# Cross-attention and FP4 feed-forward: the gated rows' lowered block reciprocals computed by ScalarE instead of GpSimd

## What is computed

```python
def fp4_quant_dequant(x):                       # BLOCK = 16, along the last dim
    xb = x.reshape(shape[:-1] + (shape[-1] // BLOCK, BLOCK))
    scale = jnp.max(jnp.abs(xb), axis=-1, keepdims=True) / 6.0
    scale = jnp.maximum(scale, jnp.float32(1e-12))
    xn = xb / scale
    idx = jnp.searchsorted(_MID, jnp.abs(xn))
    q = _GRID[idx] * jnp.sign(xn) * scale
    return q.reshape(shape)

def fp4_linear(x, w):
    return jnp.einsum('bsk,nk->bsn', fp4_quant_dequant(x), fp4_quant_dequant(w))

x = x + xattn(layernorm(x), ctx_1024, ...)
n = layernorm(x)
h = silu(fp4_linear(n, w_gate)) * fp4_linear(n, w_up)      # 704 gated columns
x = x + fp4_linear(h, w_down)
```

## Time and profile before

| | before |
|---|---|
| median of 3 runs | 435.14 us |
| the profiled execution | 436.2 us |
| its span | 434.4 us |
| busy: TensorE matmul / weight load | 363.0 / 277.7 us |
| busy: VectorE | 352.0 us |
| busy: ScalarE | 276.5 us |
| busy: GpSimd | 213.7 us |
| mean granted TensorE clock | 0.96 of 2.4 GHz |

### The profile page before, as it was taken

How to read it: one execution, slowest core, us unless ns; L and a number is a source line. 1 busy time by engine, 2 the same in 40 slices (tenths; PEclk the granted TensorE clock), 3 DMA queues, 4 the chain that set the end, 5 groups by cost and what they waited for, 6 DMA issues and landing times.

```text
span 434.4 us, 9451 instructions
## 1 busy us (share of the span) xinstructions
PE 363.0 (84%) x3659; PEld 277.7 (64%) x3659; DVE 352.0 (81%) x676; ACT 276.5 (64%) x869; POOL 213.7 (49%) x249
## 2 busy tenths in 40 slices
PE   1875698899989989999899876887884998898956
PEld 1554464677868868777687755755563766666844
DVE  2889867896987969969889798579679899999791
ACT  3657769888897897879978867265142345443331
POOL 3364323354463544544545534035543878787741
PEclk9986699999999999999999999999699799999998
DMA  7970000000000000000000000000000000000010
GB/s 215 322 273 1 2 2 0 2 3 2 2 2 2 2 2 2 2 2 2 3 2 2 2 1 2 2 0 2 0 2 1 25 14 14 26 12 26 12 51 24
DMA packets 8445, 11.48 MB, mean 26 GB/s; under 512 B 524, under 2 KB 6352, under 8 KB 8401
## 3 DMA queue, kind: packets, MB, share of 16 engines
q1 hardware_dynamic: 8401, 10.88, 7.8%
HBM read 8.78 MB, written 2.10 MB: 25 GB/s over the span
## 4 chain that ended last, share of the span: by engine, by line
DVE 36%; PE 28%; ACT 28%; issue 4%; DMA 2%; POOL 1%; SPq 0%; POOLq 0%; DVEq 0%; ACTq 0%
ACT arena L744 14%; PE ps L397 8%; PE ps L398 7%; PE ps L399 7%; ACT arena L735 4%; ACT pT L753 4%; DVE arena L1055 4%; DVE negmax L995 4%; DVE arena L1053 3%; DVE arena L986 3%; DVE pT L1004 2%; DVE arena L1179 2%; DVE blk_h L1020 2%; DVE arena L1145 2%; DMA arena<-in_L_xattn_proj_k_dram 2%
## 5 line engine op out<-in xcount | busy, mean ns | idle before, releaser
L744 ACT ACTIVATE arena<-ps,negmax 128x154 f32<-128x154 f32 x256 | 98.4, 430 | 16.4 <-DVE negmax L995 16.4
L1231 POOL TENSOR_TENSOR arena<-arena,rinv 128x104 f32<-128x104 f32 x64 | 23.1, 362 | 115.9 <-DVE rinv L1000 115.9
L1232 POOL TENSOR_TENSOR arena<-arena,rinv 128x512 f32<-128x512 f32 x64 | 66.7, 1042 | 0.0
L1004 DVE TENSOR_TENSOR pT<-ps,pT 128x512 f16<-128x512 f32 x80 | 54.6, 682 | 13.0 <-ACT pT L753 12.9
L744 ACT ACTIVATION_READ_ACCUMULATOR arena<-ps,negmax 128x1 f32 x256 | 63.4, 248 | 0.0
L543 PE MATMUL ps<-ident,arena 128*128 128x128 f32 x320 | 52.8, 288 | 4.0 <-DVE pT L1004 3.9
L753 ACT ACTIVATE pT<-ps 128x512 f16<-128x512 f32 x80 | 51.5, 644 | 6.5 <-PE ps L543 6.4
L397 PE MATMUL ps<-arena,xnT_h 128*128 128x352 f16 x128 | 41.5, 324 | 11.8 <-DVE xnT_l L1063 10.1
L995 DVE TENSOR_REDUCE negmax<-ps 128x4 f32<-128x616 f32 x64 | 50.2, 785 | 0.7 <-PE ps L533 0.5
L397 PE MATMUL ps<-arena 128*128 128x256 f16 (+2 forms) x120 | 36.6, 305 | 14.9 <-DVE arena L899 6.2
L533 PE MATMUL ps<-kT_h,arena 64*128 64x154 f16 x512 | 38.3, 235 | 12.3 <-ACT arena L744 11.6
(11 more groups left out here) (150 smaller groups left out, 1041.6 us busy)
## 6 DMA issues: line engine op xcount, KB each, us to landing
out_dram<-arena SPq DMA_DIRECT2D x16, 128.0 KB, 1.7
xs<-in_x_dram SPq DMA_DIRECT2D x2, 512.0 KB, 7.3
arena<-in_L_xattn_w_out_dram SPq DMA_DIRECT2D x1, 1024.0 KB, 11.8
xs<-in_x_dram SPq DMA_DIRECT2D x2, 384.0 KB, 6.7
wffn<-in_L_ffn_w_down_dram SPq DMA_DIRECT2D x1, 704.0 KB, 9.2
wffn<-in_L_ffn_w_gate_dram SPq DMA_DIRECT2D x1, 640.0 KB, 7.8
wffn<-in_L_ffn_w_up_dram SPq DMA_DIRECT2D x1, 640.0 KB, 8.2
arena<-in_ctx_dram SPq DMA_DIRECT2D x1, 308.0 KB
```

Of the source, the lines that this page charges most:

```text
L744: last = act.activation(prob[:, s, h * L:(h + 1) * L], ps[:, 2 * (j % 2) + k % 2, (k // 2) * L:(k // 2 + 1) * L], ACT.Exp, bias=negmax[:, ...
L1004: dve.tensor_tensor(quad_T(1, i, s, g), ps[:, T_BANK + (s + g) % 2, :].rearrange("p (c n) -> p c n", c=4), quad_T(0, i, s, g), ALU.subtrac ...
L1231: pool.tensor_tensor(rests[:, s, 4 * j:4 * j + 4, 0:REST], v[:, :, P:L], r.to_broadcast([P, 4, REST]), ALU.mult)
L1232: pool.tensor_tensor(v[:, :, 0:P], v[:, :, 0:P], r.to_broadcast([P, 4, P]), ALU.mult).then_inc(normed, 1)
```

## The change

The small product of the gated tiles' reciprocals by `BELOW` leaves GpSimd and becomes a copy with a scale on ScalarE, between `magnitude_h(t-1)` and `h_high(t-3)`. It waits for `hscaled`, and GpSimd now waits for `hlowered` alone. The products for the normalised rows and for the weights stay on GpSimd.

```diff
+            def lowered_h(i, s):
+                t = 2 * i + s
+                act.wait_ge(hscaled, 3 * t + 3)
+                act.activation(blk_h[:, s, 3], blk_h[:, s, 2], ACT.Copy, scale=BELOW).then_inc(hlowered, 1)
+
             def h_high(i, s):
...
                     if exists(shift(i, s, -1)[0]): magnitude_h(*shift(i, s, -1))
+                    if not last_tile(i, s): lowered_h(i, s)
                     if exists(turned[0]): h_high(*turned)
                     if exists(summed[0]): y_copy(*summed)
...
             def value(v, src, r, scaled, lowered, valued, t):
 
-                pool.wait_ge(scaled, 3 * t + 3)
-                pool.tensor_tensor(r[3], r[2], below[:, :].to_broadcast([P, r[2].shape[1]]), ALU.mult).then_inc(lowered, 1)
+                if scaled is not None:
+                    pool.wait_ge(scaled, 3 * t + 3)
+                    pool.tensor_tensor(r[3], r[2], below[:, :].to_broadcast([P, r[2].shape[1]]), ALU.mult).then_inc(lowered, 1)
                 pool.wait_ge(lowered, t + 1)
                 pool.tensor_tensor(blocks(v), blocks(src), spread(r[3]), ALU.mult).then_inc(valued, 1)
...
-                value(h_tmp[s][0], hid[:, s], [blk_h[:, s, r] for r in range(4)], hscaled, hlowered, hvalued, t)
+                value(h_tmp[s][0], hid[:, s], [blk_h[:, s, r] for r in range(4)], None, hlowered, hvalued, t)
```

## The result

The changed kernel takes 441.37 us (median of 4 runs, 440.08 to 443.2) against 435.13 us before (4 runs): a ratio of 1.0154, 95% interval 1.0117 to 1.0191. The forecast was 441.3 us, the range 438.3 to 443.6. The change makes the kernel slower by 1.5%, though it takes 15 instructions off GpSimd and adds 15 x 0.24 us to an engine that is idle a third of the time.

The account below looks back on a forecast made before the run. VectorE was taken to set the steady pace, TensorE to bind in tiles 12 to 14. Terms 4.1 + 0.1 + 2.0 = +6.2 us on the median of 435.14 gave 441.3 us, range 438.3 to 443.6.

Parts of the forecast that it names:

- The turn between L1053 and L1055: Steady bodies: GpSimd's large product, ready earlier, takes this gap; L1055 on 704 columns takes 1.96 us instead of 0.89.
- What comes back: Tiles 6 to 11: of L1055's 1.07 us delay, 0.40 returns behind s = 0 tiles, 0.38 behind s = 1; net +4.1 us.
- The race at L1022: Behind s = 0 tiles: GpSimd's add_x1 goes first; rival, L1022 wins, saving 0.58 us in three bodies, 439.6 us, chance 0.17.
- The tail: Tiles 12 to 14: TensorE is the bound, so late L1179 delays down by 1.07 us in tile 12, 0.9 in 14; +2.0.
- Tiles 0 to 5: Nothing at tiles 0, 1, 2, 4 and 5, net +0.1 us at tile 3.
- VectorE's idle time as cover: At tile 5 VectorE idles afterwards, so L1055's delay there was costed at nothing.
- ScalarE's queue: Rival: ScalarE held longer at the copy, so L1179 and down wait; 443 to 444 us, chance 0.10.
- GpSimd might come too late: Rival: the large product misses the gap after L1053, L1055 goes first as before; 434.6 us, chance 0.11.
- the price of the small product in the gap: Between L1053 and L1055: the small product costs L1055 some 0.06 us, 0.89 against L1053's 0.83.

Follow-up runs that it names:

- e2: The change without any lowering of the gated rows' reciprocals: GpSimd's large product takes the reciprocals themselves, nothing added on ScalarE; 440.16 us, ratio 1.0119.
- e3: The change with ScalarE's copy moved to the end of its body and made to wait for L1053 (hsummed); 431.48 us, ratio 0.9952.
- e7: The change with GpSimd's large product on 704 columns cut into two of 352; 437.09 us, ratio 1.0058.
- e1: The kernel before, GpSimd's small product kept, plus the same ScalarE copy at the change's place into an unread column; 435.73 us, ratio 1.0006.
- e6: The change with ScalarE's copy moved to the end of its body, without a wait for L1053; 441.22 us, ratio 1.015.
- e4: The kernel before with GpSimd's addition add_x1 put ahead of round_h in each body; 431.29 us, ratio 0.9911.
- e10: The kernel of e4 run once more, on the same chip as e9; 431.24 us, ratio 0.9923.
- e5: e3 and e4 together: the copy at the end of its body behind L1053, and add_x1 ahead of round_h; 430.53 us, ratio 0.9908.
- e8: e6 with the copy's wait for L1053 added for tile 4 alone; 440.55 us, ratio 1.0126.
- e9: The kernel of e5 run once more, on the same chip as e10; 430.71 us, ratio 0.9915.

## Why the prediction was right

**The turn between L1053 and L1055.** The copy took 0.24 us (forecast 0.23), the large product started 0.35 us behind the reciprocal (364.30 to 364.65; forecast 0.37), while L1053 ran, and L1055 took 1.95 us (1.96): right in each part. e2 shows the same loss with no ScalarE in it, e3 takes it away by the moment alone, e7 scales it with the length of GpSimd's instruction. That a waiting engine is blocked for the other's whole instruction and no bandwidth is shared is what the Trainium skill states (SBUF, State Buffer, section "Who interferes with whom"); e7's 1.35 us for half the columns, with GpSimd's total no smaller (208.1 against 197.9 us), agrees.

**What comes back.** Net of it, 0.67 us behind an s = 0 tile and 0.69 behind an s = 1 tile were forecast. The changed kernel has 7.90 us from `scales_h` of tile 8 to that of tile 9 against 7.23 before, and 8.56 against 7.88 for the next: +0.67 and +0.68. Tiles 6 to 12: 49.42 against 45.31 us, +4.11, forecast +4.1.

**The race at L1022** went to GpSimd in all three steady bodies, as in the earlier trace rows: 0.75 us each. But between tiles 4 and 5 it went the other way in the changed kernel: L1028 took 0.38 us, since `round_h` began 0.46 us behind L1061 and not 0.15 as before. That stretch came out 0.41 us shorter than before, where I had put nothing. Had it gone as in the other three, some 0.4 us more would have been lost. Why `round_h` was late there, no run settles.

**The tail** was forecast at +2.0 and measured at +2.11 from tile 12 to the end (43.42 against 41.31 us). The two waits of TensorE shown above are 1.86 of it: 1.10 us in tile 12 (forecast 1.07), 0.76 in tile 14 (0.9). The clock has no part in it, since it is 1.00 in tiles 12 to 14 and 0.92 over the last 21 us of both kernels. The other 0.25 is a longer busy time of TensorE in the records, 31.9 against 31.6 us; what it is made of stays open.

**Tiles 0 to 5:** forecast +0.1 in all; measured +0.07 from tile 0 to 3, +0.26 from tile 3 to 4, -0.41 from 4 to 5, +0.28 from 5 to 6: +0.20 together, right in the sum rather than one by one. At tile 3 I had let more come back behind L1055 than did. At tile 5 I had counted on VectorE's idle time as cover, but TensorE is busy throughout that body in both kernels (8.95 of 8.95 us before, 9.23 of 9.23 after), at a granted clock of 0.82; how it comes to take 0.28 us more no run settles. That the small terms nearly cancel is luck.

**The rivals.** ScalarE's queue is refuted by e1 and e6. That GpSimd might come too late was the right opposite case, and e3 is that case; but the time given for it was off. I had read 0.06 us of L1055's 0.89 as the price of the small product in the gap. In e3 no small product is there and L1055 still takes 0.89: it is the instruction's own time when it starts behind a finished one. And I hadn't looked at the layer norm, where a late product saves 1.1 us more.

## What to carry to other kernels

Where VectorE's instructions with two SBUF inputs alternate with GpSimd's, look at who is waiting at each end of an instruction: the gap between two dependent ones of VectorE is a turn, and it goes to whatever GpSimd instruction stands ready, for its whole length. Taking a short GpSimd instruction out of such a place can let a long one in; before making GpSimd earlier, look at what it will then collide with, and gate it, shorten its instructions or put the short ones where VectorE must wait anyway. Here one row of the old trace, L1055 at 1.96 us in one body of fifteen, held the answer.

## What the runs showed of the hardware that I had not expected

- A 4-number addition of VectorE (128x4) took 1.28 us instead of 0.16, because GpSimd's product had started 0.12 us before it; and that alone set off 1.1 us of idle TensorE.
- In tile 4 TensorE stands idle, and its granted clock falls from 2.4 to 1.2 GHz (1.00 to 0.50 in the rows) about when it starts again, for a time that differs by kernel. In windows of 1 us it stands at 0.50 from 336 to 342 us before, and in e3 only from 333 to about 336. The next body had 0.81 or 0.82 on the mean behind an idle stretch of 4.6 to 5.2 us (before, the change, e1, e2, e4, e6, e7, e10), and 0.94 to 0.98 behind one of 3.5 to 3.6 us (e3, e5, e8, e9).
- At the end of the kernel the idle stretch alone doesn't tell. It is 3.15 or 3.16 us in e3, before, the change, e6 and e8 alike, and the last 21 us have a clock of 0.99, 0.92, 0.92, 0.92 and 0.84. Between e3 and before, with equal matmuls, that goes with 1.4 us. In e8, where one wait at tile 4 was added to e6, the end, some 90 us later, takes 0.81 us more; what carries it there stays open.
